# A layer-normed graph convolution in split fp32: two buffers of hi and lo instead of three, deeper load buffers, and the subtractions of a slot behind its additions

## The reference, cut to what matters

```python
h = jnp.maximum(_layernorm(x, axis=-1), 0.0)         # x: 4096 x 256
rowsum = adj.sum(axis=1)                             # adj: 4096 x 4096
d = jnp.where(rowsum > 0, rowsum ** (-0.5), 0.0)
support = (d[:, None] * adj * d[None, :]) @ h
out = x + relu(support @ W + b)                      # W: 256 x 256
```

## Time and profile before

| | before |
|---|---|
| median of 3 runs | 409.94 us (409.82 to 417.97) |
| the profiled execution | 411.25 us |
| its span | 409.2 us |
| mean granted TensorE clock | 0.994 |
| TensorE busy | 390.9 us, 96% of the span |
| VectorE busy | 311.0 us, 76% |
| ScalarE busy | 292.1 us, 71% |
| moved by DMA | 147.39 MB, 360 GB/s |

### The profile page before, as it was taken

One profiled execution on the slowest core, in us unless ns is written; L12 is line 12 of the kernel. 1 busy time (PEld: TensorE's weight loads), 2 busy tenths in 40 slices (PEclk: granted clock), 3 DMA queues, 4 the chain that ended last, 5 costly groups with the idle time before them and its releaser, 6 DMA issues.

```text
span 409.2 us, 5151 instructions
## 1 busy us (share of the span) xinstructions
PE 390.9 (96%) x1760; PEld 324.3 (79%) x1760; DVE 311.0 (76%) x314; ACT 292.1 (71%) x285; POOL 115.7 (28%) x271
## 2 busy tenths in 40 slices
PE   3999799999999999999999999999999999999991
PEld 3888687888888888888888888888888888887771
DVE  5757668878797878869585987869386987929996
ACT  2799868887888888597776778876677793445622
POOL 3343525242422362332132521433023360000000
PEclk9999999999999999999999999999999999999997
DMA  8999999999999999999999989999899991097656
GB/s 286 424 418 362 421 421 422 422 419 421 420 422 422 419 420 421 400 388 425 420 421 361 356 315 389 422 421 422 322 336 360 343 362 70 24 400 295 202 170 243
DMA packets 22472, 147.39 MB, mean 360 GB/s; under 512 B 2608, under 2 KB 2864, under 8 KB 6064
## 3 DMA queue, kind: packets, MB, share of 16 engines
q1 hardware_dynamic: 22448, 147.07, 90.0%
HBM read 142.87 MB, written 4.19 MB: 359 GB/s over the span
## 4 chain that ended last, share of the span: by engine, by line
PE 69%; DMA 12%; DVE 7%; issue 5%; ACT 5%; SPq 1%; ACTq 0%; DVEq 0%
PE moved L685 17%; PE moved L686 17%; PE moved L687 17%; DMA at<-in_adj_t 6%; DMA nat<-in_adj 6%; PE held L685 5%; PE held L686 5%; PE held L687 5%; PE moved L655 3%; DVE acc L551 2%; DVE lo L536 1%; DVE acc L566 1%; DVE nat L572 1%; ACT hi L352 1%; ACT G L364 1%
## 5 line engine op out<-in xcount | busy, mean ns | idle before, releaser
L352 ACT ACTIVATE hi<-at,s 128x1024 fp32r<-128x1024 f32 x112 | 123.0, 1146 | 46.6 <-issue 33.3
L532 DVE SCALAR_TENSOR_TENSOR lo<-at,s,hi 128x1024 fp32r<-128x1024 f32 x112 | 141.1, 1279 | 17.9 <-ACT hi L352 17.9
L685 PE MATMUL moved<-hi,G 128*128 128x512 f32 x384 | 150.1, 391 | 3.0 <-DVE acc L548 2.1
L686 PE MATMUL moved<-lo,G 128*128 128x512 f32 x384 | 149.5, 389 | 0.0
L687 PE MATMUL moved<-hi,G 128*128 128x512 f32 x384 | 149.4, 389 | 0.0
L551 DVE TENSOR_TENSOR acc<-moved,acc 128x1024 f32<-128x1024 f32 x84 | 102.7, 1223 | 53.3 <-PE moved L687 53.2
L339 ACT ACTIVATE nat<-nat 128x2048 f32<-128x2048 f32 x64 | 122.3, 1912 | 12.1 <-DMA nat<-in_adj 12.1
L685 PEld LDWEIGHTS moved<-hi,G 128*128 128x128 f32 x384 | 72.1, 188 | 20.5 <-DVE acc L551 3.2
L687 PEld LDWEIGHTS moved<-hi,G 128*128 128x128 f32 x384 | 72.1, 188 | 15.1
L686 PEld LDWEIGHTS moved<-lo,G 128*128 128x128 f32 x384 | 72.1, 188 | 14.6
L462 POOL TENSOR_TENSOR row_sum<-part 128x1 f32<-128x1 f32 x32 | 16.4, 511 | 170.5 <-ACT nat L339 170.4
(11 more groups left out here) (57 smaller groups left out, 228.4 us busy)
## 6 DMA issues: line engine op xcount, KB each, us to landing
nat<-in_adj SPq DMA_DIRECT2D x64, 1024.0 KB, 10.3
at<-in_adj_t SPq DMA_DIRECT2D x64, 1024.0 KB, 10.6
nat<-in_x_t SPq DMA_DIRECT2D x6, 512.0 KB, 4.1
out<-nat SPq DMA_DIRECT2D x5, 512.0 KB, 5.1
at<-in_x SPq DMA_DIRECT2D x4, 512.0 KB, 5.6
turned<-in_x SPq DMA_DIRECT2D x3, 512.0 KB, 14.1
turned<-in_x_t SPq DMA_DIRECT2D x2, 512.0 KB, 5.2
out<-turned SPq DMA_DIRECT2D x2, 512.0 KB, 5.0
```

The costliest lines, as they stand in the source:

```text
L352: nc.scalar.activation(hi[g % RING][:, 2 * c:2 * c + 2, :], at[g % LA][:, 2 * c:2 * c + 2, :], ACT.Copy, scale=s[:, j:j + 1]).then_inc(hi_ ...
L532: nc.vector.scalar_tensor_tensor(out=lo[g % RING][:, tiles, :], in0=at[g % LA][:, tiles, :], scalar=s[:, j:j + 1], in1=hi[g % RING][:, til ...
L685: nc.tensor.matmul(into[:, f, :], big, hi[g % RING][:, t, :], start=begins, stop=False)
L686: nc.tensor.matmul(into[:, f, :], big, lo[g % RING][:, t, :], start=False, stop=False)
```

## The change

`hi` and `lo` get two buffers each instead of three, `at` five instead of four, `nat` four instead of three. On ScalarE the copies of the d rows move from behind `round_slot(58)` to before it. On VectorE both gathers of a narrow slot come before both subtractions.

```diff
-    LN = 3
-    LA = 4
-    RING = 3
+    LN = 4
+    LA = 5
+    RING = 2
...
                 for m in NATS[g]:
                     sum_nat(m)
+                if k == LAST and q == 0:
+                    for r in range(NP // 2):
+                        take_d_rows(r)
                 if g + 2 < len(SLOTS):
                     round_slot(g + 2)
...
                 if k == LAST:
                     if q == 0:
                         act.wait_ge(b_landed, DMA)
-                        for r in range(NP // 2):
-                            take_d_rows(r)
...
                 if NARROW[k] and NARROW[SLOTS[g + 2][0]]:
                     for p in range(2):
                         gather(k, 2 * q + p)
-                        subtract(g + 2, p)
+                    for c in range(2):
+                        subtract(g + 2, c)
```

## The result

| | before | after |
|---|---|---|
| median of the runs | 410.79 us (4 runs) | 450.33 us (449.99 to 450.90, 4 runs) |
| the profiled execution | 411.25 us | 450.47 us |
| its span | 409.2 us | 448.5 us |
| mean granted clock | 0.994 | 0.963 |

The changed kernel is slower: ratio 1.0977, 95% interval 1.0946 to 1.1008. The forecast was 438.0 and the range ended at 446. The direction and, as will be seen, every gap are as forecast; the time lies where the first rival had it, at 443 to 452.

What follows compares the result with a forecast made beforehand. TensorE was taken to bound the kernel (busy 390.9 of 409.2 us), VectorE the last step. Terms -2.4 + 24.4 + 3.8 + 2.35 = +28.1 us took the profiled 411.25 to 439.4, median 438.0; range 433 to 446.

Steps and rivals of the forecast that it cites:

- the first rival: TensorE's clock falls in the new gaps: 443 us if in the two long ones, 452 if in all six; chance 0.20.
- The plain slot stays at 5.44: Narrow slots without extra work keep 5.44 us, the next gather having 0.2 us of slack: 0, bounds to 3 us.
- The early stall goes: Slots 2 and 6: TensorE no longer waits for gathers held behind lo of slot 3; gain 2.4 us, bounds 0 to 2.7.
- The copies come too late: Copies out of a moved pair stall TensorE after slots 20, 28, 40, 44 (3.5 us each), 24 and 32 (5.2 each): +24.4.
- VectorE's extras: Statistics in slot 12, centring in 16 and 36, make_G in 52, behind lo and ahead of an urgent gather: +3.8 us.
- The last step: From s, slot 56's start: late G and rounds waiting for hi start lo of slot 63 later; +2.35 us, bounds 1 to 7.
- The clock: Half rate behind TensorE's gaps, 2.4 us for each cold start; left out of the sum as a rival, chance 0.20.
- From the profiled execution to the median: The last step of the sum: 1.3 us taken off the profiled execution's 439.4 to forecast a median of 438.0.

Runs made afterwards that it cites:

- old_order: The changed kernel (two buffers) with VectorE's order put back to gather, subtract, gather, subtract in narrow slots; 481.72 us.
- order_alone: The kernel before, three buffers and rings kept, with only VectorE's order changed: both gathers of a narrow slot ahead of both subtractions; 409.21 us.
- copies_first: The changed kernel with ScalarE's copies out of the moved pair (take_turned, round_raw, take_product) ahead of the rounding of slot g + 2; 431.09 us.
- copies_rest_first: As copies_first, with rest_of_raw on VectorE ahead of the subtractions too; 417.58 us.
- all_first: As copies_rest_first, with VectorE's statistics and centring ahead of the subtractions too; 412.35 us.
- two_repaired: As all_first, with make_G of slot 52 ahead of the subtractions and, in the last step, VectorE's gather ahead of its subtract; 409.41 us.
- shallow_loads: The changed kernel with the load rings as before (3 of rows, 4 of blocks); 450.64 us.
- copy_between: The changed kernel with take_turned and take_product between the two pieces of the rounding instead of behind both; 446.19 us.
- filled_gaps: The changed kernel with unread matmuls added in TensorE's six gaps, twelve in each short one and nineteen in each long one; 439.76 us.
- half_filled: As filled_gaps, with five matmuls instead of twelve in the short gaps and ten instead of nineteen in the long ones; 445.63 us.

## Why the prediction was right and where it was wrong

*The plain slot stays at 5.44*: right. Slots without an extra take 5.44 in the trace after too, so the 0.2 us of slack was there, and old_order shows that the reordering is what keeps it. One figure of the working is a slip: a gather must end by 5.44 + 0.23 - 0.39 = 5.28, not 5.22; the later terms use the 0.22 us of slack that this gives.

*The early stall goes*: right in size (-2.45 for -2.4). The rows of the kernel after, ACT and DVE (they answer to the earlier trace rows), have both gathers of slot 1 before lo of slot 3, and hi of slot 3 at 42.92, where I had 42.7:

```profile
42.92 2.18 ACT L352 ACTIVATE hi<-at,s 128x1024 fp32r<-128x1024 f32 x2
...
40.61 1.22 DVE L549 COPY acc<-moved 128x1024 f32<-128x1024 f32 x1
42.42 1.23 DVE L549 COPY acc<-moved 128x1024 f32<-128x1024 f32 x1 [0.59 <-PE moved L689]
44.09 2.48 DVE L533 SCALAR_TENSOR_TENSOR lo<-at,s,hi 128x1024 fp32r<-128x1024 f32 x2 [0.44 <-ACT hi L352]
```

order_alone adds that with three buffers and the shallower load rings some of this gain (0.4 of 2.7 us in its trace) is lost to the loads.

*The copies come too late*: right in place, releaser and length. 3.4 us four times and 5.1 twice; copies_first and copies_rest_first removed just these, and came to 431.1 and 417.6 where 431.5 and 417.6 were expected.

*VectorE's extras*: right, 3.8 for 3.8; all_first and two_repaired removed them but for some 0.5 us.

*The last step*: +1.8 for +2.35. The rounds are as worked out (TensorE starts slots 59 to 62 at s + 21.4, 27.3, 33.8 and 39.7; forecast 21.5, 27.4, 33.9, 39.9), and lo of slot 63 starts at 430.64, s + 41.57 for 41.75. The rest is in the tail, from there to the end, which is 0.4 shorter than before. two_repaired, which changed the last step and make_G together, came 2.9 us below all_first by the medians and 2.3 by the ratios (2.8 expected). In its trace slot 53, held by make_G before, is 0.8 shorter, and slots 58 to 61 are 3.3 shorter together; but the first slot starts 0.6 later and the work behind TensorE's last matmul takes 1.6 longer, so the span gains 1.8. The kernel after, DVE, where the wait for hi at the head of a round shows (answers to the earlier trace rows):

```profile
418.25 2.29 DVE L537 TENSOR_TENSOR lo<-at,hi 128x2048 fp32r<-128x2048 f32 x1 [0.57 <-ACT hi L347]
420.46 1.22 DVE L573 TENSOR_TENSOR turned<-acc,turned 128x1024 f32<-128x1024 f32 x1
421.60 1.22 DVE L552 TENSOR_TENSOR acc<-moved,acc 128x1024 f32<-128x1024 f32 x1
```

*The clock*: this is the step that failed. I had its mechanism and its price (2.4 us a gap; measured 11.4 over five gaps, 2.3 each), but gave it one chance in five and left it out of the sum, and ended the range at two gaps. The reason I gave was that the clock at the end of the trace still stood at full 3 us after the last matmul, so that the short gaps "may be free of it". One event had been read as if it were a threshold. It was none: where the gaps were left unfilled, behind those of 5.1 us the clock was lowered every time (ten of ten), behind those of 3.4 eleven times in twelve (after, shallow_loads, old_order), and behind those of 2.3 in copy_between three times in four. The rule of the Trainium skill that I had weighed, "TensorE: Matmul & The Clock Gate", "Why this matters for your kernels", that such gaps between bursts in mid-kernel cost the rate behind them as well, was right here and should have been in the sum: 28.1 + 11.4 = 39.5, where the spans of the two profiled executions differ by 39.3. The runs show it even for gaps of 2.3 us, which are shorter than those that the table warns of.

*From the profiled execution to the median*: a small step that also failed. The sum gave 439.4 us for the profiled execution, and filled_gaps, which has everything but the clock, took 439.69 in its own. The forecast of 438.0 took off another 1.3, by which the profiled execution of the kernel before stood above its median; in the kernel after and in filled_gaps the two agree within 0.15 us.

## What to carry to other kernels

When a ring loses a buffer, look at which wait of which engine now moves to "the end of this very step", and then at everything that stands behind that wait in the same queue; if the engine that would end the step needs any of it, move it ahead of the wait. Here three such moves, without any memory, took the loss from 9.8% to 0.5%, and two more to nothing. A stall of TensorE of more than two microseconds between dense matmuls should be priced as its length and a stretch at half rate behind it, here 1.6 to 2.9 us, unless a run shows otherwise.

## What the runs showed of the hardware that I had not expected

The clock is lowered behind gaps much shorter than the trace of before suggested: of 2.34 us (three of four in copy_between), while a gap of 2.2 us before and gaps of 1.2 in old_order left it alone. It can fall after TensorE is at work again (in copy_between restart at 207.70 and half clock from about 208.2, and behind slot 44 restart at 319.50 and half clock from about 320.8). In the last step of copy_between a wait of 2.65 us was followed by it too, 1.3 us after the restart. Gaps of the same length do not all do it: that of slot 44 did not in the kernel after and did in shallow_loads, and repeated runs of one kernel differ by it (copy_between 442.2 and 446.5; half_filled 443.8 and 448.1, at clocks 0.983 and 0.971). Every low stretch ahead of the tail lasted 3.4 or 6.8 us by the granted clock. What decides between them was not tried and stays open.
